# Front of a transformer tower: the patch stage one tile further ahead, two banks for turned queries and keys, the patch weights' sum by products

## The chip, the cores and the metric

The kernel runs on one core of one Trainium2 chip. The metric is the device time of one execution in microseconds (us). The core's engines are TensorE (PE in the profile; PEld is its weight load), VectorE (DVE), ScalarE (ACT), GpSimd (POOL) and SyncE (SP), which issues the DMAs. Each works through its own queue in order; semaphores order them among each other.

## The reference, cut to what matters

32 images of 96x96 are cut into 36 patches each. Patches are normalised, projected to 256 numbers, normalised again and given a position; with two class tokens an image has 38 tokens. Then come attention with ternary weights, a mixture of experts, attention in integers and three blocks with quantised weights. The change is in the first part and the first attention's projection:

```python
x = layernorm(x, ln1_g, ln1_b)                     # 1152 patches x 768
x = einsum('bhwp,pd->bhwd', x, W) + bias           # x 256
x = layernorm(x, ln2_g, ln2_b) + pe
h = concatenate([cls_tok, cls_token + cls_pos, x])
qkv = layernorm(h) @ ternary_weight(w_qkv).T
q, k = rms_norm(q), rms_norm(k)
q, k = rotary(q) * q_gain, rotary(k)
... softmax(q k^T) v, then @ ternary_weight(w_proj).T, the experts, the second layer
```

## The kernel before, in words

The tokens are 10 tiles of 128 (`NT`), the patches the first 9 of them (`TOK`). Item 0 of the second part is the tile of class tokens (`Z_TILE[0]` is tile 9), item n is tile n - 1. Normalisations are folded into weights: the patch weights, scaled by ln1's gain (`patch_c`), are centred by subtracting the mean over all 768 rows. VectorE adds the six row blocks up (`patch_total`), TensorE multiplies the total by ones (`patch_sums`, after 12 passes that sum ln1's bias rows), VectorE subtracts (`patch_weights`). VectorE also rounds the ternary weights, those of qkv first (`ternary_rounded(0)`, `ternary_made(0)`) and those of the output projection at the end of the front (part 1).

A patch tile t then goes this way: TensorE turns it (`patches_turned`, L621), ScalarE copies it to SBUF (`patches_kept`), TensorE projects it (`patches_projected`, L629, 12 passes into bank `Y`), VectorE makes y and its statistics (`y_stats`, L409), GpSimd the inverse root and shift (`y_rstd`, L579), ScalarE normalises (`normalised`, L733), GpSimd multiplies by the gain and adds the position (`placed`, L585 and L588: h is made). `embedded(part)` (L574) adds the bias row to three tiles of the position table; x's own statistics are `x_stats` and `x_rstd`.

Item n goes on: TensorE turns h (`rows_turned`), ScalarE copies (`rows_kept`), TensorE projects (`projected`, L650), ScalarE takes the values and the squares (`values`, `squared`), VectorE sums the squares and rotates (`z_rotated`, L431 first), GpSimd adds the rotated halves (`rotation_added`, L569), ScalarE takes the root (`rooted`), VectorE inverts and scales (`row_factor`, `row_scaled`), TensorE turns the row (`heads_turned`, L658, into bank `QK`), and ScalarE lays it out by image (`by_image`, L769 and L771). `h_stats` and `h_rstd` (L565) are the statistics of h.

Each engine has a loop written out by hand, `for i in range(NT + 1)`. In turn i it does the patch work of tile i, `rows_turned` to `squared` of item i, and `z_rotated` to `by_image` of item i - 1; turns 0 and 1 are special. The order in TensorE's turn is `patches_projected(i)`, `rows_turned(i)`, `patches_turned(i + 1)`, `projected(i)`, `heads_turned(i - 1)`. Scores of the first attention (L863) wait for `by_image` of the last item. Before the first load has landed, the engines have only memsets and ScalarE's table load.

## Time and profile before

| what | us |
|---|---|
| median of three runs (lowest, highest) | 539.51 (535.71, 540.89) |
| the profiled execution, device time | 536.86 |
| its span, first to last instruction | 535.0 |
| TensorE busy, share of the span | 412.5, 77% |
| VectorE busy | 315.0, 59% |
| ScalarE busy | 244.9, 46% |
| GpSimd busy | 155.0, 29% |
| mean granted TensorE clock, share of full | 0.865 |

The front is the first 93.8 us of the span. Durations and times of day below are of the profiled execution. Windows were read for the clock that TensorE was granted, timelines for who waits for whom; "[idle 2.15 <- ACT front L771]" on a row says that the engine stood still for 2.15 us ahead of it and that ScalarE's line 771 released it.

### The profile page before, as it was taken

To read this page: it belongs to the slowest core of one execution; us is meant where nothing else is said; L and a number is where in the kernel's file an instruction comes from. 1 tells how busy PE (TensorE), PEld (TensorE's weight loads), DVE (VectorE), ACT (ScalarE), POOL (GpSimd) and SP (SyncE) were. 2 spreads that over 40 slices of the span, in tenths; PEclk is the share of its full clock that TensorE was granted. 3 is DMA by queue.
4 is the path that set the end of the run, shared out by engine and by line. 5 is a ranking of instruction groups with operands and counts; after the bars stand their busy time and mean duration, and the time that the engine had idled before them with its cause. 6 is when DMAs were issued, how large, how long until landed. Compare 5 with 4: busy or idle time off the path is not lost.

```text
span 535.0 us, 9515 instructions
## 1 busy us (share of the span) xinstructions
PE 412.5 (77%) x3499; PEld 303.6 (57%) x3499; DVE 315.0 (59%) x846; ACT 244.9 (46%) x519; POOL 155.0 (29%) x191
## 2 busy tenths in 40 slices
PE   5678883577798999999889995532796147699997
PEld 3556652466687866665556783211343135589996
DVE  4977877789472311323321228669898997636643
ACT  4245544365745212222112212693298478566651
POOL 3485773689320610000000054008010001213310
PEclk9898997599988999999999998685555556999999
DMA  8941111970015140111110081000000000000002
GB/s 270 401 177 17 23 23 20 374 337 3 2 45 222 69 147 21 39 58 44 39 39 31 21 308 45 0 1 2 1 2 0 1 4 2 1 1 2 1 20 75
DMA packets 19793, 38.64 MB, mean 72 GB/s; under 512 B 2136, under 2 KB 16164, under 8 KB 18340
## 3 DMA queue, kind: packets, MB, share of 16 engines
q1 hardware_dynamic: 18788, 35.41, 19.2%
q0 software_dynamic: 960, 2.62, 1.4%
q8 instruction: 29, 0.48, 0.4%
q14 instruction: 16, 0.13, 0.1%
HBM read 29.77 MB, written 7.01 MB: 69 GB/s over the span
## 4 chain that ended last, share of the span: by engine, by line
PE 51%; DVE 24%; ACT 11%; issue 6%; POOL 4%; DMA 2%; DVEq 0%; SPq 0%; ACTq 0%; POOLq 0%
PE psum L1314 11%; PE psum L1346 5%; PE psum L1321 5%; PE psum L2406 4%; PE psum L2439 3%; PE psum L1360 3%; PE psum L985 2%; DVE ring L905 2%; ACT experts L1722 2%; PE psum L2445 2%; DVE att_den L912 2%; PE psum L1338 1%; DMA front<-expert_results,slot_of 1%; PE psum L2423 1%; DVE att_max L908 1%
## 5 line engine op out<-in xcount | busy, mean ns | idle before, releaser
L1314 PE MATMUL psum<-experts,ring 128*128 x136 | 64.3, 596 | 1.9 <-issue 1.2
L1138 DVE TENSOR_TENSOR ring<-ring,psum 128x512 f32<-128x512 f32 x17 | 11.7, 688 | 62.8 <-PE psum L1314 62.8
L1245 POOL DMA_INDIRECT front<-expert_results,slot_of x10 | 9.7, 974 | 125.0 <-DMA expert_results<-ring 122.2
L1321 PE MATMUL psum<-front,shared 128*128 128x256 f32 (+1 forms) x160 | 36.3, 382 | 0.0
L1314 PEld LDWEIGHTS psum<-experts,ring 128*128 128x128 f32 x136 | 23.3, 190 | 19.4 <-issue 19.4
L1321 PEld LDWEIGHTS psum<-front,shared 128*128 128x128 f32 x160 | 30.4, 197 | 3.7
L1346 PE MATMUL psum<-experts,ring 128*128 x136 | 32.1, 379 | 0.0
L1346 PEld LDWEIGHTS psum<-experts,ring 128*128 128x128 f32 x136 | 25.8, 190 | 10.3 <-issue 7.7
L2406 PE MATMUL psum<-experts 128*128 128x256 f32 (+1 forms) x120 | 27.5, 372 | 4.6 <-ACT experts L2469 4.6
L629 PE MATMUL psum<-experts,ring 128*128 128x256 f32 x108 | 27.6, 409 | 2.6 <-DVE ring L409 2.6
L1444 ACT COPY ring<-psum 128x512 f32<-128x512 f32 x17 | 10.0, 586 | 42.3 <-PE psum L1338 42.3
L2406 PEld LDWEIGHTS psum<-experts 128*128 128x128 f32 x120 | 21.8, 190 | 7.6 <-ACT experts L2469 5.4
L1430 ACT COPY ring<-psum 128x256 f32<-128x256 f32 x17 | 6.3, 372 | 42.8 <-PE psum L1330 42.8
L629 PEld LDWEIGHTS psum<-experts,ring 128*128 128x128 f32 x108 | 21.6, 206 | 6.4 <-issue 3.0
L873 PE MATMUL psum<-tab,experts 128*128 128x128 f32 x128 | 18.8, 295 | 6.4 <-ACT ring L935 6.3
L2479 ACT ACTIVATE ring<-psum,ffn_first_b 128x256 f32<-128x256 f32 (+1 forms) x30 | 12.3, 459 | 24.8 <-PE psum L2406 24.8
L2380 POOL TENSOR_TENSOR ffn_rs<-ffn_var,minus_half 128x2 f32<-128x2 f32 x15 | 10.4, 693 | 44.7 <-DVE ffn_var L2324 44.7
L1360 PE MATMUL psum<-shared,ring 128*128 128x256 f32 (+1 forms) x80 | 20.0, 405 | 3.8 <-DVE ring L1143 3.8
L2174 POOL TENSOR_TENSOR rstd<-out_var,minus_half 128x2 f32<-128x2 f32 x5 | 4.0, 796 | 63.4 <-DVE out_var L2135 63.4
L841 POOL TENSOR_TENSOR ring<-ring,att_max 128x608 f32<-128x608 f32 x16 | 19.3, 1209 | 7.1 <-DVE att_max L908 6.3
L1143 DVE TENSOR_TENSOR ring<-ring,psum 128x512 f32<-128x512 f32 (+1 forms) x10 | 6.6, 661 | 24.9 <-PE psum L1321 24.9
L846 POOL TENSOR_TENSOR experts<-experts,att_inv 128x608 f32<-128x608 f32 x16 | 19.4, 1211 | 2.3 <-DVE att_inv L916 2.3
(364 smaller groups left out, 1072.2 us busy)
## 6 DMA issues: line engine op xcount, KB each, us to landing
experts<-in_experts SPq DMA_DIRECT2D x8, 1536.0 KB, 12.1
experts<-in_x SPq DMA_DIRECT2D x9, 384.0 KB, 8.3
expert_rows<-zeros SPq DMA_DIRECT2D x1, 2176.0 KB, 14.6
ring<-expert_rows SPq DMA_DIRECT2D x17, 128.0 KB, 2.1
shared<-in_shared SPq DMA_DIRECT2D x1, 1536.0 KB, 17.7
experts<-in_ffn_q SPq DMA_DIRECT2D x1, 1536.0 KB, 6.4
experts<-in_ffn_s SPq DMA_DIRECT2D x1, 1536.0 KB, 10.7
experts<-in_pos_embed SPq DMA_DIRECT2D x1, 1152.0 KB, 9.4
```

The costliest lines, as they stand in the source:

```text
L629: mm = nc.tensor.matmul(psum[:, Y, 0:D], tok_xT[t % 2][:, k, :], patch_c[:, k, :], start=(k == 0), stop=(k == KP - 1))
L841: nc.gpsimd.tensor_tensor(att_s[p % 3], att_s[p % 3], m, ALU.subtract).then_inc(s_shifted.sem, 1)
L846: nc.gpsimd.tensor_tensor(att_p[p % 3][:, :, 0:SEQ], att_p[p % 3][:, :, 0:SEQ], w, ALU.mult).then_inc(p_scaled.sem, 1)
L873: tr = nc.tensor.transpose(psum[:, 4 + c // 4, (c % 4) * P:(c % 4 + 1) * P], att_p[p % 3][:, 2 * c:2 * c + 2, :], ident)
L1138: nc.vector.tensor_tensor(o, o, up_bank(g), ALU.mult).then_inc(hidden_done.sem, 1)
L1314: mm = nc.tensor.matmul(bank, sl_xT[t % 2][:, k, :], slot_w(t, block, k, F), start=(k == 0), stop=(k == KD - 1))
L1321: mm = nc.tensor.matmul(o[:, b, 0:w], shared_w(block, k, (2 * half + b) * P, P), moe_x(c)[:, k, 0:w], start=(k == 0), stop=(k == KD - 1))
L1346: mm = nc.tensor.matmul(psum[:, 2, 0:D], sl_hT[t % 2][:, k, :], slot_w(t, 2, k, D), start=(k == 0), stop=(k == KF - 1))
L1360: mm = nc.tensor.matmul(psum[0:m, 3, u * D:(u + 1) * D], sh_h[c % 2][:, k, u * P:u * P + m], shared_w(2, k, 0, D), start=(k == 0), stop=(k ...
L2406: mm = nc.tensor.matmul(psum[:, n % 2, o * CHUNK:o * CHUNK + w], ffn_w[:, 2 * b, k, o * P:(o + 1) * P], ffn_xT[:, k, a:a + w], start=(k == ...
L2439: mm = nc.tensor.matmul(psum[:, 6 + n % 2, o * CHUNK:o * CHUNK + w], ffn_w[:, 2 * b + 1, k, o * P:(o + 1) * P], g[:, k, 0:w], start=(k == ...
L2479: nc.scalar.activation(ffn_sq[n % 2][:, k, 0:w], psum[:, n % 2, k * CHUNK:k * CHUNK + w], ACT.Square, bias=ffn_first_b[:, b, k:k + 1])
```

## The change

The patch stage runs one tile further ahead. In turn i the engines now do the patch work of tile i + 1 (`patches_projected`, `y_stats`, `y_rstd`, `placed`, `normalised`) and turn tile i + 2, beside the items i and i - 1 as before. The turns 0 and 1 are written out. Turned queries and keys have two banks, 5 and 7, so that `heads_turned(n)` waits for `by_image(n - 2)` and not n - 1; the turned weights of the output projection go to bank 4. The patch weights' total is made in three sums of two blocks, one addition on VectorE, and TensorE adds the three up with products by ones. `embedded` has parts of 1, 2, 3 and 3 tiles instead of 3 x 3: the first waits for the ternary rounding of qkv, the others stand behind `x_rstd(2)`, `x_rstd(3)` and the end of turn 3. ScalarE begins with one square root of zeros. Nothing behind the front is changed.

```diff
@@ -343,7 +343,7 @@
...
         v_row = view(ring, 3840, 4, 2, KV_HEADS, 2, HD)
-        patch_t = tok_yn[1]
+        patch_t = view(ring, PATCH_DIM, KP // 2, D)
         x_mv, x_var, x_rs = sb("x_mv", [P, TOK, 2]), sb("x_var", [P, TOK]), sb("x_rs", [P, TOK])
...
@@ -368,8 +368,9 @@
...
         Z_TILE = [NT - 1] + list(range(NT - 1))
-        XT, Y, HT, Z, QK = 0, 2, 3, [4, 6], 5
-        TERN_QKV, TERN_PROJ, SUM, ROW = 6, 7, 7, 6
+        XT, Y, HT, Z, QK = 0, 2, 3, [4, 6], [5, 7]
+        TERN_QKV, TERN_PROJ, SUM, ROW = 6, 4, 7, 6
+        POS_PARTS = [range(0, 1), range(1, 3), range(3, 6), range(6, TOK)]
         TERN_COLS, TERN_GROUPS = [slice(0, 3 * D), slice(3 * D, 5 * D)], [slice(0, 12), slice(12, 20)]
...
@@ -490,7 +491,7 @@
...
                 dve.wait_ge(patch_scaled.sem, patch_scaled.done(0))
-                nc.vector.tensor_reduce(patch_t, patch_c.rearrange("p k d -> p d k"), AX.X, ALU.add).then_inc(patch_totaled.sem, 1)
+                nc.vector.tensor_tensor(patch_t, patch_c[:, 0:KP // 2, :], patch_c[:, KP // 2:KP, :], ALU.add).then_inc(patch_totaled.sem, 1)
 
...
@@ -524,26 +525,28 @@
...
             patch_rows()
-            for i in range(NT + 1):
+            y_stats(0)
+            ternary_made(0)
+            x_stats(1)
+            dve.wait_ge(cls_made.sem, cls_made.done(0))
+            h_stats(NT - 1)
+            x_stats(2)
+            y_stats(1)
+            qkv_weights()
+            h_stats(0)
+            y_stats(2)
+            x_stats(3)
+            for i in range(2, NT + 1):
                 for n in z_items(i - 1):
                     z_rotated(n)
-                if i == 1:
-                    dve.wait_ge(cls_made.sem, cls_made.done(0))
-                    h_stats(NT - 1)
-                    y_stats(i)
-                if 1 <= i <= TOK:
+                if i <= TOK:
                     h_stats(i - 1)
...
                     row_factor(n)
-                if i < TOK and i != 1:
-                    y_stats(i)
+                if i + 1 < TOK:
+                    y_stats(i + 1)
                 for n in z_items(i - 1):
                     row_scaled(n)
-                if i == 0:
-                    ternary_made(0)
-                    x_stats(1)
-                if i == 1:
-                    qkv_weights()
                 if i + 2 < TOK:
...
@@ -571,8 +574,9 @@
...
                 pool.wait_ge(l_pe.sem, l_pe.all)
-                nc.gpsimd.tensor_tensor(pos_embed[:, 3 * part:3 * part + 3, :], pos_embed[:, 3 * part:3 * part + 3, :],
-                                        rows[:, 1:2, :].to_broadcast((P, 3, D)), ALU.add).then_inc(pos_ready.sem, 1)
+                r = POS_PARTS[part]
+                nc.gpsimd.tensor_tensor(pos_embed[:, r[0]:r[-1] + 1, :], pos_embed[:, r[0]:r[-1] + 1, :],
+                                        rows[:, 1:2, :].to_broadcast((P, len(r), D)), ALU.add).then_inc(pos_ready.sem, 1)
 
...
@@ -584,30 +588,38 @@
...
                 pool.wait_ge(yn_scaled.sem, yn_scaled.done(t))
-                pool.wait_ge(pos_ready.sem, pos_ready.done(t // 3))
+                pool.wait_ge(pos_ready.sem, pos_ready.done([t in r for r in POS_PARTS].index(True)))
                 nc.gpsimd.tensor_tensor(h[:, t, :], tok_yn[t % 2], pos_embed[:, t, :], ALU.add).then_inc(h_made.sem, 1)
...
             x_rstd(0)
+            y_rstd(0)
+            pool.wait_ge(tern_ready.sem, tern_ready.done(0))
             embedded(0)
-            for i in range(NT + 1):
+            x_rstd(1)
+            placed(0)
+            h_rstd(NT - 1)
+            x_rstd(2)
+            embedded(1)
+            y_rstd(1)
+            placed(1)
+            h_rstd(0)
+            y_rstd(2)
+            placed(2)
+            x_rstd(3)
+            embedded(2)
+            for i in range(2, NT + 1):
                 for n in z_items(i - 1):
                     rotation_added(n)
-                if i == 1:
-                    h_rstd(NT - 1)
-                    y_rstd(i)
-                if 1 <= i <= TOK:
+                if i <= TOK:
                     h_rstd(i - 1)
-                if i < TOK and i != 1:
-                    y_rstd(i)
-                if i < TOK:
-                    placed(i)
-                if i == 0:
-                    x_rstd(1)
+                if i + 1 < TOK:
+                    y_rstd(i + 1)
+                    placed(i + 1)
                 if i + 2 < TOK:
                     x_rstd(i + 2)
-                if i in (0, 1):
-                    embedded(1 + i)
+                if i == 3:
+                    embedded(3)
             for u in range(3):
...
@@ -652,10 +664,10 @@
...
                 pe.wait_ge(row_made.sem, row_made.done(t))
-                if t >= 1:
-                    pe.wait_ge(qkT_ready.sem, qkT_ready.done(t - 1))
+                if t >= 2:
+                    pe.wait_ge(qkT_ready.sem, qkT_ready.done(t - 2))
                 for c in range(3):
-                    tr = nc.tensor.transpose(psum[:, QK, c * P:(c + 1) * P], qk_row[t % 2][:, c * P:(c + 1) * P], ident)
+                    tr = nc.tensor.transpose(psum[:, QK[t % 2], c * P:(c + 1) * P], qk_row[t % 2][:, c * P:(c + 1) * P], ident)
                 tr.then_inc(qkT_turned.sem, 1)
...
@@ -688,32 +700,35 @@
...
                 pe.wait_ge(patch_totaled.sem, patch_totaled.done(0))
-                nc.tensor.matmul(psum[:, SUM, 0:D], ones, patch_t, start=True, stop=True).then_inc(patch_summed.sem, 1)
+                for k in range(KP // 2):
+                    mm = nc.tensor.matmul(psum[:, SUM, 0:D], ones, patch_t[:, k, :], start=(k == 0), stop=(k == KP // 2 - 1))
+                mm.then_inc(patch_summed.sem, 1)
 
...
             patches_turned(0)
-            for i in range(NT + 1):
-                if i < TOK:
-                    if i == 0:
-                        patches_turned(1)
-                        pe.wait_ge(patch_centred.sem, patch_centred.done(0))
-                    patches_projected(i)
-                if i == 1:
-                    ternary_turned()
-                    rows_turned(0)
-                    ternary_summed()
-                    patches_turned(2)
-                    pe.wait_ge(qkv_centred.sem, qkv_centred.done(0))
-                    projected(0)
-                    rows_turned(1)
-                    projected(1)
-                elif i < NT:
-                    if i >= 2:
-                        rows_turned(i)
-                        if i + 1 < TOK:
-                            patches_turned(i + 1)
-                        projected(i)
+            pe.wait_ge(patch_centred.sem, patch_centred.done(0))
+            patches_projected(0)
+            patches_turned(1)
+            patches_projected(1)
+            ternary_turned()
+            rows_turned(0)
+            patches_turned(2)
+            ternary_summed()
+            patches_projected(2)
+            patches_turned(3)
+            pe.wait_ge(qkv_centred.sem, qkv_centred.done(0))
+            projected(0)
+            rows_turned(1)
+            projected(1)
+            for i in range(2, NT + 1):
+                if i + 1 < TOK:
+                    patches_projected(i + 1)
+                if i < NT:
+                    rows_turned(i)
+                    if i + 2 < TOK:
+                        patches_turned(i + 2)
+                    projected(i)
                 for n in z_items(i - 1):
...
@@ -764,7 +779,7 @@
...
                 s = slice(POS_TILE * t, POS_TILE * t + n)
-                bank = psum[:, QK, 0:QK_ROW].rearrange("p (c s i) -> p c s i", c=3, s=POS_TILE)[:, :, 0:n, :]
+                bank = psum[:, QK[item % 2], 0:QK_ROW].rearrange("p (c s i) -> p c s i", c=3, s=POS_TILE)[:, :, 0:n, :]
                 q_out = q_im[:, :, 0:IMAGES * SEQ].rearrange("p b (i s) -> p b s i", s=SEQ)[:, :, s, :]
...
@@ -776,6 +791,8 @@
...
 
+            act.wait_ge(zeros_ready.sem, zeros_ready.done(0))
+            nc.scalar.activation(qkv_sd[:, 0, :], zeros[:, 0:HK], ACT.Sqrt)
             act.wait_ge(l_patch_w.sem, l_patch_w.all)
...
@@ -785,31 +802,31 @@
...
             patches_kept(0)
-            for i in range(NT + 1):
+            patches_kept(1)
+            normalised(0)
+            ternary_taken(0)
+            rows_kept(0)
+            patches_kept(2)
+            normalised(1)
+            patches_kept(3)
+            values(0)
+            squared(0)
+            rows_kept(1)
+            normalised(2)
+            values(1)
+            squared(1)
+            for i in range(2, NT + 1):
                 for n in z_items(i - 1):
                     rooted(n)
-                if i < 2:
-                    if i == 1:
-                        ternary_taken(0)
-                        rows_kept(0)
-                    patches_kept(i + 1)
-                    normalised(i)
-                if i == 1:
-                    values(0)
-                    squared(0)
-                    rows_kept(1)
-                    values(1)
-                    squared(1)
-                if i >= 2:
-                    for n in z_items(i):
-                        rows_kept(n)
-                    if i + 1 < TOK:
-                        patches_kept(i + 1)
-                    if i < TOK:
-                        normalised(i)
-                    for n in z_items(i):
-                        values(n)
-                        squared(n)
+                if i < NT:
+                    rows_kept(i)
+                if i + 2 < TOK:
+                    patches_kept(i + 2)
+                if i + 1 < TOK:
+                    normalised(i + 1)
+                if i < NT:
+                    values(i)
+                    squared(i)
                 for n in z_items(i - 1):
...
             ternary_taken(1)
```

## Rows read from the trace of the kernel before

**Rows 1.** Timeline, one steady turn: start us, us, engine, line, operation [idle before <- releaser].
```profile
55.65 2.76 PE L629 MATMUL psum<-experts,ring 128*128 128x256 f32 x12
...
56.98 0.49 DVE L431 TENSOR_REDUCE qkv_ss<-experts 128x20 f32<-128x320 f32 x1 [0.40 <-ACT experts L752]
...
59.12 1.53 PE L650 MATMUL psum<-qkv_w,ring 128*128 128x384 f32 x4
...
59.40 0.48 DVE L409 SCALAR_TENSOR_TENSOR ring<-psum,x_rs,rows 128x256 f32<-128x256 f32 x1
...
60.83 0.71 POOL L579 TENSOR_TENSOR y_rs<-y_var,minus_half 128x1 f32<-128x1 f32 x1 [0.72 <-DVE y_var L416]
...
61.94 0.60 ACT L733 ACTIVATE ring<-ring,y_shift,y_rs 128x256 f32<-128x256 f32 x1 [1.77 <-POOL y_shift L581]
...
63.11 0.49 DVE L431 TENSOR_REDUCE qkv_ss<-experts 128x20 f32<-128x320 f32 x1 [0.41 <-ACT experts L752]
```

**Rows 2.** Windows: us, busy of PE, PEld, DVE, ACT, POOL, granted clock, DMA, GB/s.
```profile
42.50:43.40 0.90, 0.84 (x4) 0.87 (x5) 0.86 (x5) 0.00 (x0) 0.90 (x3) 0.50 0.11 30
...
56.10:62.20 6.10, 5.36 (x28) 4.08 (x27) 5.40 (x23) 3.59 (x12) 4.50 (x8) 1.00 0.17 23
```

**Rows 3.** Timeline, VectorE's L431 and TensorE around the third turn.
```profile
35.07 0.49 DVE L431 TENSOR_REDUCE qkv_ss<-experts 128x20 f32<-128x320 f32 x1 [1.35 <-ACT experts L752]
...
41.67 0.49 DVE L431 TENSOR_REDUCE qkv_ss<-experts 128x20 f32<-128x320 f32 x1
...
42.56 0.87 PE L658 MATMUL psum<-tab,ring 128*128 128x128 f32 x3 [2.15 <-ACT front L771]
...
43.23 3.89 PE L629 MATMUL psum<-experts,ring 128*128 128x256 f32 x12
...
50.86 0.48 DVE L431 TENSOR_REDUCE qkv_ss<-experts 128x20 f32<-128x320 f32 x1 [0.41 <-ACT experts L752]
```

**Rows 4.** Timeline, the front's last turns and the first scores.
```profile
81.47 0.48 DVE L431 TENSOR_REDUCE qkv_ss<-experts 128x20 f32<-128x320 f32 x1 [1.77 <-ACT experts L752]
...
83.47 2.93 PE L650 MATMUL psum<-qkv_w,ring 128*128 128x384 f32 x4 [0.46 <-ACT ring L739]
...
93.76 0.81 PE L863 MATMUL psum<-front 32*64 32x76 f32 x32 [0.79 <-ACT front L771]
```

**Rows 5.** Groups of instructions by form, 0 to 95 us: busy us, mean ns | idle before.
```profile
L569 POOL TENSOR_TENSOR experts<-experts 128x320 f32<-128x320 f32 x10 | 8.6, 863 | 7.1 <-DVE experts L436 7.1
...
L588 POOL TENSOR_TENSOR h<-ring,experts 128x256 f32<-128x256 f32 x9 | 6.6, 728 | 0.7
...
L574 POOL TENSOR_TENSOR experts<-experts,rows 128x768 f32<-128x768 f32 x3 | 5.8, 1918 | 3.5 <-DMA experts<-in_pos_embed 3.5
...
L565 POOL TENSOR_TENSOR rstd<-var_eps,minus_half 128x1 f32<-128x1 f32 x10 | 5.7, 568 | 0.0
...
L471 DVE TENSOR_SCALAR experts<-experts 128x512 int16<-128x512 bf16 x1 | 0.3, 294 | 0.0
```

**Rows 6.** Timeline, the start of the front.
```profile
8.78 2.78 DVE L493 TENSOR_REDUCE ring<-experts 128x256 f32<-128x1536 f32 x1 [1.36 <-ACT experts L781]
...
11.70 0.67 PE L691 MATMUL psum<-ring,tab 128*128 128x256 f32 x2
...
12.83 2.07 DVE L499 SCALAR_TENSOR_TENSOR experts<-psum,experts 128x256 f32<-128x256 f32 x6
...
17.08 2.13 POOL L574 TENSOR_TENSOR experts<-experts,rows 128x768 f32<-128x768 f32 x1 [3.46 <-DMA experts<-in_pos_embed]
...
17.58 1.84 DVE L471 TENSOR_SCALAR experts<-experts 128x768 int16<-128x768 bf16 x1
...
19.79 0.48 DVE L409 SCALAR_TENSOR_TENSOR ring<-psum,x_rs,rows 128x256 f32<-128x256 f32 x1
...
20.42 4.29 PE L629 MATMUL psum<-experts,ring 128*128 128x256 f32 x12 [2.61 <-DVE ring L409]
...
24.81 0.15 DVE L401 TENSOR_SCALAR x_var<-x_mv 128x1 f32<-128x1 f32 x1
```

## The prediction

> **What bounds the kernel now.** I read the chain of waits first: it goes through every stage, and the diff touches none behind the front. So the change is worth what it moves the moment at which attention can start, the first score product at 93.76 us of the span of 535.0 us. I take everything behind it to shift by the same amount.
>
> Then I read the timeline of one steady turn. I mark a turn by VectorE's reduction L431, the first instruction of `z_rotated(n)`, and call it z(n). z(4) is at 56.98, z(5) at 63.11: a turn is 6.13 us, and the chain in it is closed. From z(4) VectorE works 2.42 us (rotation, `h_stats`, `row_factor`) until `y_stats` starts (L409). 1.43 us later GpSimd starts y's power (L579), after 1.11 more ScalarE can normalise (L733), and behind that in its queue stand `values` and `squared`, whose end releases z(5) 1.17 later: 2.42 + 1.43 + 1.11 + 1.17 = 6.13 [rows 1]. VectorE is busy 5.40 of 6.10 us, TensorE 5.36, GpSimd 4.50 in 8 instructions [rows 2].
>
> Two places are off this beat. z(2) to z(3) is 50.86 - 41.67 = 9.19 us, 3.06 more than a turn: the second `heads_turned` waits 2.15 us for its only bank, which ScalarE is still emptying, and behind that pause the projection L629 takes 3.89 us [rows 3] instead of 2.76 [rows 1]. The granted clock was 0.50, its lower level, as the wait ended [rows 2]. And the tail, where little is left to overlap: z(8) at 81.47, scores at 93.76 [rows 4].
>
> **The change, part by part.**
>
> *Steady turn: 0.* In turn i the patch work of tile i+1 stands where that of i stood, and on every engine the kinds of work keep their order. `squared(i)` is still behind a normalisation, which waits for GpSimd, which waits for VectorE in the same turn: the 6.13 us chain is as long as before. x's factor is now made only one turn ahead; its power ends before the 2.42 us at which `y_stats` wants it, since GpSimd's work behind z is `placed`'s rest and one power (0.73 + 0.57) [rows 5].
>
> *Two banks: -2.9.* The 2.15 us wait goes, and with it the pause that the slow projection followed: -3.06 for z(2) to z(3), and +0.14 as both `by_image` now stand ahead of `rooted(2)` on ScalarE. If the projection stays slow though the wait goes, about -2.0; the lower end is 0, where ScalarE's queue and not the bank holds the turn.
>
> *Patch weights' sum: +0.5.* VectorE's strided reduction took 2.78 us, but TensorE came to its product only at 11.70, behind the row products, just as the reduction ended [rows 6]. So a quicker addition releases nobody, whatever it takes below 2.78. TensorE now makes three products, four more passes. A pass of this width is 2.76/12 = 0.23 us in a steady projection [rows 1], 0.36 in the slow one at 20.42 [rows 6]: +0.9 to +1.4. I take 0.9, since L691's two passes took 0.67 in all, so its end goes from 12.37 to 13.3. L499 started at 12.83, when VectorE came free [rows 6]; now at 13.35.
>
> *GpSimd out of the way of the rounding: -1.4.* L471 with 768 elements took 1.84 us [rows 6], with 512 elements 0.29 [rows 5], which makes 0.44 for 768. While the long one ran, GpSimd was in `embedded(0)`, from 17.08 to 19.21 [rows 6]; the short one ran alone. Now `embedded(0)` waits for `tern_ready`. The bounds are 0 and -1.4.
> The Trainium skill (SBUF — State Buffer, Terms) says that VectorE and GpSimd arbitrate for one port pair, held to the end of an instruction. By that rule L471 stood still until GpSimd's addition was over, which these rows agree with; were the width alone at work, the term would be 0 and the total 1.4 us later.
>
> With both, x's statistics for tile 1, which ended at 24.96 [rows 6], end at about 24.1.
>
> *GpSimd's queue in the new prologue: +1.6.* Here I see the gain go. The embedding additions (3 x 1.92 us [rows 5]) were made where no chain hung on GpSimd for long. Now they stand, as 1, 2, 3 and 3 tiles, between the steps of the y chain. From 24.1, with a power 0.57, `h_rstd` with its small product 0.8, `placed` twice 0.73 and a gap 1.5, a rotation 0.87, three tiles 1.81, two tiles 1.25 (between 0.73 and 1.81) [rows 5], y's pair 1.0 and ScalarE's normalisation 0.65 (1.11 and 0.60 with their gaps [rows 1]): x(1) 0.57, placed(0) 1.5, h(9) 0.8, x(2) 0.57, two tiles 1.25, y(1) 1.0, ScalarE 0.65, placed(1) 1.5, h(0) 0.8, y(2) 1.0, ScalarE 0.65, placed(2) 1.5, x(3) 0.57, three tiles 1.81, two rotations 1.74, h(1) 0.8, y(3) 1.0. That is 17.71; with a few gaps y(3)'s shift is ready at 42.0, and z(2) comes 1.17 behind the normalisation's start, at 43.2 against 41.67.
> TensorE alone would be sooner. It has one patch projection more ahead of z(1), +2.76; it starts its prologue 0.9 earlier, and the projection at 20.42 took 4.29 us behind a pause [rows 6] which is now shorter: 2.76 - 0.9 - 1.4 = +0.5. z(1) would be at 35.6, and VectorE goes from z(1) to z(2) in 6.6 us [rows 3]: z(2) at 42.2. The slower of the two queues counts.
>
> *embedded(3), at the end of turn 3: +1.1.* It puts 1.81 us between x's power and `rotation_added(3)`. GpSimd is idle for 0.72 us ahead of L579 in a turn [rows 1], so y(5) is 1.81 - 0.72 = 1.1 late, and all behind it. The bounds are 0 and 1.8.
>
> *Tail: -0.8.* In turn 8 no y work is left: z(8) needs `rows_kept(8)`, the projection and ScalarE's two squares. In a steady turn that projection starts 2.14 us behind z (59.12) [rows 1]; here no patch projection is ahead of its turned rows, and I take 1.7. It took 1.53 us there [rows 1] and 2.93 after a thin stretch [rows 4]. TensorE will have had about 0.9 us of work in the 4 us ahead of it, so I take 2.93, and 0.7 for the squares (1.17 less the normalisation's share): 1.7 + 2.93 + 0.7 = 5.33 instead of 6.13. Bounds: -0.4 with 2.14, -2.2 at the high clock. From z(8) to the scores it is 12.29 us [rows 4], VectorE's own work with the rounding of the last weights first, then one tile alone: as before.
>
> *ScalarE's early square root: 0.* The table load ahead of the first `rooted` lay beside VectorE's rotation and `h_stats`; it goes under the wait for the weights, with one small activation.
>
> **The sum.** z(2) +1.6 (which has the first two terms of the start in it); banks -2.9: z(3) at 49.6, -1.3; embedded(3) +1.1: z(4) at 56.8, -0.2; tail -0.8: scores at about 92.8. In all **-1.0**. The profiled execution took 536.86 us with its span of 535.0, so 535.9 by its own account. It lies 2.65 below the median of the three runs, 539.51; all four have a mean of 538.24. I put the forecast on that: 537.2.
>
> **The rivals.**
> 1. *GpSimd's queue hides after all*, its instructions lying under other waits: z(2) +0.5, banks -2.9, embedded(3) 0, tail -0.8 to -2.2: -3.2 to -4.6, so 533.6 to 535.0. For it: GpSimd is idle 1.6 us of a turn [rows 2]. Against: the additions come as one piece of 1.81.
> 2. *Slower, by TensorE's new order.* `projected(0)` and `projected(1)` stand behind `patches_projected(2)` and `patches_turned(3)`. At the lower level the two patch projections there cost 1.1 to 1.5 more each and the two of h 1.4 each, some 5.2 us, of which 1.1 is hidden beside GpSimd's queue (43.2 against 42.2); the total is -1.0 + 4.1 = +3.1, 541.3. It turns the sign from a delay of 2.1 us on. For it: a projection right behind a pause was slow twice [rows 3, 6]. Against: the pauses there are now about 1 us.
> 3. *The bank did not hold turn 3*: ScalarE's two `by_image` do. The total is -1.0 + 2.9 = +1.9, 540.1. Against: the row names what TensorE waited for, the bank's last reader [rows 3], and with a second bank nothing else is ahead of that transpose.
>
> **How the numbers follow.** The forecast's case has 0.50 (535.7 to 538.7), rival 1 0.27, rival 2 0.13, rival 3 0.10. About 1%, 5.4 us, is what a measurement of this kernel can tell from no change. No case reaches it alone. Faster by over 1% needs rival 1 with the high clock in the tail and some more: 0.13; slower by over 1% needs rivals 2 and 3 together: 0.06; within 1%: 0.81. The range reaches from rival 1 with a fast execution to rival 2: 532.5 to 541.0.
>
> **What the profile after would show.** L471 at 768 elements near 0.44 us; the first L409 at 18.9; no wait of L658 for ScalarE and z(2) to z(3) near 6.3; z(2) near 43.2, with GpSimd hardly idle from 24 to 42; z(3) to z(4) near 7.2, the other turns 6.13; z(7) to z(8) near 5.3; scores near 92.8. The prediction is wrong if z(2) is ahead of 42.5 or behind 45, if z(3) to z(4) is 6.1, or if a stage behind the scores changes its length by over 1 us.

## The result, and the profile after

The changed kernel takes 533.19 us (median of 9 runs, 530.27 to 535.75) against 537.87 (9 runs, 535.71 to 540.89); the ratio is 0.9917, 95% interval 0.9892 to 0.9941. So it is faster by 0.8%, 3 to 6 us. Its profiled execution took 535.75 us with a span of 533.9, its slowest run: one pair of executions shows 1.1 us, the medians 4.7. How far that can be accounted for is told below.

| moment in the front, us | before | forecast | after |
|---|---|---|---|
| first `y_stats` | 19.79 | 18.9 | 18.14 |
| z(2) | 41.67 | 43.2 | 41.76 |
| z(3) | 50.86 | 49.6 | 47.89 |
| z(4) | 56.98 | 56.8 | 54.88 |
| z(8) | 81.47 | 80.5 | 77.76 |
| z(9) | 88.60 | - | 84.89 |
| first scores | 93.76 | 92.8 | 90.06 |

The scores start 3.70 us earlier, not 1.0. Line numbers have moved: L431 is now L432, L409 L410, L471 L472, L499 L500, L574 L578, L579 L583, L629 L641, L650 L662, L658 L670, L691 L704, L739 L754, L752 L767, L771 L786, L863 L880; in the variants below a line can be off by one or two more.

The start of the front, timeline of the changed kernel (start us, us, engine, line, operation, idle before); it answers to [rows 6]:

```profile
10.94 1.27 PEld L704 LDWEIGHTS psum<-ring,tab 128*128 128x128 f32 x6
...
11.15 1.46 PE L704 MATMUL psum<-ring,tab 128*128 128x256 f32 x6
...
12.65 2.08 DVE L500 SCALAR_TENSOR_TENSOR experts<-psum,experts 128x256 f32<-128x256 f32 x6 [1.46 <-PE psum L704]
...
17.41 0.36 DVE L472 TENSOR_SCALAR experts<-experts 128x768 int16<-128x768 bf16 x1
...
18.14 0.48 DVE L410 SCALAR_TENSOR_TENSOR ring<-psum,x_rs,rows 128x256 f32<-128x256 f32 x1
...
22.03 0.73 POOL L578 TENSOR_TENSOR experts<-experts,rows 128x256 f32<-128x256 f32 x1 [0.54 <-DVE experts L482]
...
23.16 0.15 DVE L402 TENSOR_SCALAR x_var<-x_mv 128x1 f32<-128x1 f32 x1
...
25.98 2.83 PE L641 MATMUL psum<-experts,ring 128*128 128x256 f32 x12 [1.02 <-DVE ring L410]
```

VectorE's sum is ready before TensorE gets to the three products, and `patch_weights` (L500) waits 1.46 us for them, yet starts at 12.65 against 12.83. The rounding L472 takes 0.36 us instead of 1.84. The second patch projection takes 2.86 us at 19.24, the third 2.83: no slow one, where [rows 6] has 4.29.

GpSimd's additions (L578) and y's power (L583) in the new prologue, VectorE's L444 and L422 beside them, and the two transposes L670:

```profile
26.67 1.26 POOL L578 TENSOR_TENSOR experts<-experts,rows 128x512 f32<-128x512 f32 x1
...
35.40 1.82 POOL L578 TENSOR_TENSOR experts<-experts,rows 128x768 f32<-128x768 f32 x1
35.43 0.42 DVE L422 BATCH_NORM_STATS2 hst<-h 128x6 f32<-128x256 f32 x1
...
36.47 0.79 DVE L444 TENSOR_TENSOR qkv_rg<-qkv_rg,gain 128x20 f32<-128x20 f32 x1
...
39.55 0.56 POOL L583 TENSOR_TENSOR y_rs<-y_var,minus_half 128x1 f32<-128x1 f32 x1
...
39.95 1.08 PE L670 MATMUL psum<-tab,ring 128*128 128x128 f32 x6 [1.67 <-DVE ring L458]
...
41.76 0.49 DVE L432 TENSOR_REDUCE qkv_ss<-experts 128x20 f32<-128x320 f32 x1
```

GpSimd waited three times 0.72 us for ScalarE's normalisation between 24 and 42, 2.2 us in all, and for nothing else. L444 is a product of 128x20 that takes 0.18 us in a steady turn; here it takes 0.79, until the addition at 35.40 is over. Not every VectorE instruction is held: L422 at 35.43 took its usual 0.42 us beside the same addition. The six passes of the transposes now run together and wait for VectorE's row alone; the wait of 2.15 us for ScalarE in [rows 3] is gone.

Turn 3 to 4, and the tail; they answer to [rows 1] and [rows 4]:

```profile
47.89 0.48 DVE L432 TENSOR_REDUCE qkv_ss<-experts 128x20 f32<-128x320 f32 x1 [0.41 <-ACT experts L767]
...
49.42 1.80 POOL L578 TENSOR_TENSOR experts<-experts,rows 128x768 f32<-128x768 f32 x1
...
50.19 1.07 DVE L444 TENSOR_TENSOR qkv_rg<-qkv_rg,gain 128x20 f32<-128x20 f32 x1
...
52.75 0.57 POOL L583 TENSOR_TENSOR y_rs<-y_var,minus_half 128x1 f32<-128x1 f32 x1
...
54.88 0.48 DVE L432 TENSOR_REDUCE qkv_ss<-experts 128x20 f32<-128x320 f32 x1 [0.41 <-ACT experts L767]
```

```profile
73.25 0.49 DVE L432 TENSOR_REDUCE qkv_ss<-experts 128x20 f32<-128x320 f32 x1 [1.77 <-ACT experts L767]
...
74.79 2.25 PE L662 MATMUL psum<-qkv_w,ring 128*128 128x384 f32 x4 [2.49 <-ACT ring L754]
...
77.76 0.49 DVE L432 TENSOR_REDUCE qkv_ss<-experts 128x20 f32<-128x320 f32 x1 [1.35 <-ACT experts L767]
...
84.89 0.48 DVE L432 TENSOR_REDUCE qkv_ss<-experts 128x20 f32<-128x320 f32 x1
...
90.06 0.81 PE L880 MATMUL psum<-front 32*64 32x76 f32 x32 [0.80 <-ACT front L786]
```

z(2) to z(3) is 6.13 us (9.19 in [rows 3]), z(3) to z(4) 6.99, the turns after it 6.12, turn 8 4.51, z(8) to z(9) 7.13 and from there to the scores 5.17.

What I had not looked at is TensorE in the prologue. The windows of the changed kernel, then those of the kernel before (us, busy of PE, PEld, DVE, ACT and POOL with counts, granted clock, DMA share, GB/s):

```profile
15.00:31.00 16.00, 13.99 (x72) 10.57 (x71) 14.67 (x47) 4.97 (x11) 9.17 (x14) 1.00 1.06 411
...
31.00:45.00 14.00, 11.43 (x56) 8.78 (x57) 12.10 (x46) 7.78 (x26) 12.10 (x21) 1.00 0.18 40
```

```profile
15.00:31.00 16.00, 10.99 (x45) 8.10 (x46) 15.20 (x42) 4.00 (x8) 10.39 (x14) 0.89 1.06 410
...
31.00:45.00 14.00, 10.25 (x44) 7.30 (x43) 10.25 (x42) 7.98 (x24) 10.77 (x17) 0.90 0.20 47
```

From 15 to 31 us TensorE now is busy for 13.99 us instead of 10.99 and keeps its granted clock of 1.00 up to 45 us, where before it fell to a mean of 0.89 and 0.90, that is, for a part of the time to its lower level of 1.2 GHz. The second of these falls stood behind the wait for the bank [rows 2, 3]; the first is the one that goes with the order.

### The profile page after: what moved, and what is told of

Its sections match the earlier page's. It is cut to its first block, busy times and chain, and to the rows that moved or that the text cites. A ratio compares the mean times of both kernels' runs of the same rounds, so it can differ in the third digit from the quotient of the medians.

```text
span 533.9 us, 9523 instructions
## 1 busy us (share of the span) xinstructions
PE 413.0 (77%) x3502; PEld 305.2 (57%) x3503; DVE 313.8 (59%) x846; ACT 243.6 (46%) x519; POOL 154.4 (29%) x192
## 4 chain that ended last, share of the span: by engine, by line
PE 56%; DVE 22%; ACT 11%; issue 6%; POOL 3%; DMA 1%; DVEq 0%; SPq 0%; ACTq 0%; POOLq 0%
PE psum L1331 11%; PE psum L1338 6%; PE psum L1363 6%; PE psum L2423 4%; PE psum L1377 4%; PE psum L2456 3%; PE psum L890 2%; PE psum L2462 2%; PE psum L1002 2%; PE psum L1355 1%; ACT experts L1739 1%; PE psum L2440 1%; DVE tile_peak L1767 1%; DVE front L1766 1%; PE psum L641 1%
## 5 line engine op out<-in xcount | busy, mean ns | idle before, releaser
L1331 PEld LDWEIGHTS psum<-experts,ring 128*128 128x128 f32 x136 | 23.3, 190 | 19.5 <-issue 19.4
L1363 PEld LDWEIGHTS psum<-experts,ring 128*128 128x128 f32 x136 | 25.8, 190 | 10.3 <-issue 7.6
L641 PE MATMUL psum<-experts,ring 128*128 128x256 f32 x108 | 25.1, 382 | 3.5 <-DVE experts L500 1.5
L641 PEld LDWEIGHTS psum<-experts,ring 128*128 128x128 f32 x108 | 19.9, 190 | 7.1 <-DVE experts L500 1.8
L890 PEld LDWEIGHTS psum<-tab,experts 128*128 128x128 f32 x128 | 16.1, 158 | 9.1 <-POOL experts L863 8.3
L662 PE MATMUL psum<-qkv_w,ring 128*128 128x384 f32 x40 | 17.4, 563 | 5.0 <-ACT ring L754 5.0
```

The costliest lines, as they stand in the source:

```text
L641: mm = nc.tensor.matmul(psum[:, Y, 0:D], tok_xT[t % 2][:, k, :], patch_c[:, k, :], start=(k == 0), stop=(k == KP - 1))
L662: mm = nc.tensor.matmul(psum[:, Z[n % 2], 0:QKV], qkv_hT[n % 2][:, k, :], qkv_w[:, k, :], start=(k == 0), stop=(k == KD - 1))
L890: tr = nc.tensor.transpose(psum[:, 4 + c // 4, (c % 4) * P:(c % 4 + 1) * P], att_p[p % 3][:, 2 * c:2 * c + 2, :], ident)
L1331: mm = nc.tensor.matmul(bank, sl_xT[t % 2][:, k, :], slot_w(t, block, k, F), start=(k == 0), stop=(k == KD - 1))
L1363: mm = nc.tensor.matmul(psum[:, 2, 0:D], sl_hT[t % 2][:, k, :], slot_w(t, 2, k, D), start=(k == 0), stop=(k == KF - 1))
```

## The experiments

Where no median is given, a kernel was executed once. The first loads land up to 0.3 us apart, and the weights' centring ends at different times after them, so I compare lengths within a run: first `y_stats` less `patch_weights`, turns, and so on. All marks, in us:

| kernel | patch_weights | first y_stats | z(2) | z(2) to z(3) | z(3) to z(4) | turn 8 | z(8) to z(9) | scores |
|---|---|---|---|---|---|---|---|---|
| before | 12.83 | 19.79 | 41.67 | 9.19 | 6.12 | 6.12 | 7.13 | 93.76 |
| after | 12.65 | 18.14 | 41.76 | 6.13 | 6.99 | 4.51 | 7.13 | 90.06 |
| after, again | 13.04 | 18.54 | 42.15 | 6.12 | 7.00 | 3.86 | 7.14 | 89.80 |
| one_bank | 12.78 | 18.27 | 41.86 | 10.63 | 6.99 | 5.17 | 7.14 | 95.32 |
| reduce | 12.69 | 18.17 | 41.77 | 6.11 | 7.00 | 5.17 | 7.13 | 90.70 |
| emb0_early | 13.10 | 18.98 | 42.60 | 6.13 | 6.99 | 4.20 | 7.14 | 90.59 |
| spread | 13.07 | 18.55 | 41.17 | 6.12 | 6.12 | 5.17 | 7.14 | 89.25 |
| b_two_banks | 12.64 | 19.61 | 41.49 | 6.13 | 6.12 | 6.11 | 7.14 | 90.52 |
| b_two_banks, timed | 12.87 | 19.95 | 44.96 | 6.13 | 6.12 | 6.12 | 7.14 | 94.01 |
| round_early | 13.24 | 18.74 | 42.35 | 6.12 | 7.00 | 3.75 | 5.55 | 88.82 |
| no_sqrt | 11.90 | 17.39 | 40.99 | 6.12 | 6.99 | 4.96 | 7.14 | 89.73 |
| kept_busy | 13.15 | 18.65 | 42.24 | 6.12 | 6.99 | 3.79 | 7.14 | 89.81 |
| both | 13.54 | 19.03 | 41.65 | 6.12 | 6.12 | 4.76 | 5.18 | 88.45 |
| all3 | 12.55 | 18.04 | 40.66 | 6.13 | 6.12 | 3.76 | 4.92 | 86.56 |

**One bank again in the changed kernel (one_bank).**

```diff
-        XT, Y, HT, Z, QK = 0, 2, 3, [4, 6], [5, 7]
+        XT, Y, HT, Z, QK = 0, 2, 3, [4, 6], [5, 5]
...
-                if t >= 2:
-                    pe.wait_ge(qkT_ready.sem, qkT_ready.done(t - 2))
+                if t >= 1:
+                    pe.wait_ge(qkT_ready.sem, qkT_ready.done(t - 1))
```

> The changed kernel with one bank for turned queries and keys again. My theory (the bank holds turn 3): after, z(2) 41.76 and z(3) 47.89 are 6.13 us apart; here TensorE waits about 2 us for ScalarE's last copy ahead of the second heads_turned, the projection behind it is slow, and z(2) to z(3) is again near 9 us; scores near 93.0 instead of 90.06. Rival (ScalarE's queue of two by_image holds the turn, or being a tile ahead has already covered the bank): z(2) to z(3) stays within 0.5 us of 6.13 and scores at 90 to 90.5.

z(2) to z(3) is 10.63 us, 4.50 more than with two banks, and more than the 9 I expected. The timeline shows the wait of 2.16 us, and a patch projection L641 of 5.33 us behind it, for which `y_stats` waits 3.38:

```profile
42.76 0.88 PE L670 MATMUL psum<-tab,ring 128*128 128x128 f32 x3 [2.16 <-ACT front L786]
...
43.42 5.33 PE L641 MATMUL psum<-experts,ring 128*128 128x256 f32 x12
...
48.79 0.48 DVE L410 SCALAR_TENSOR_TENSOR ring<-psum,x_rs,rows 128x256 f32<-128x256 f32 x1 [3.38 <-PE psum L641]
...
52.49 0.49 DVE L432 TENSOR_REDUCE qkv_ss<-experts 128x20 f32<-128x320 f32 x1 [0.40 <-ACT experts L767]
```

The bank held the turn. Nearly all beyond the wait is the slow projection, 2.6 us over its steady 2.75. Turn 8 is 5.17.

**Two banks alone on the kernel before (b_two_banks).**

```diff
-        XT, Y, HT, Z, QK = 0, 2, 3, [4, 6], 5
-        TERN_QKV, TERN_PROJ, SUM, ROW = 6, 7, 7, 6
+        XT, Y, HT, Z, QK = 0, 2, 3, [4, 6], [5, 7]
+        TERN_QKV, TERN_PROJ, SUM, ROW = 6, 4, 7, 6
```

(with the wait for t - 2 and the bank by item, as in the change)

> The kernel before with two banks for turned queries and keys and nothing else. Theory (the bank is worth 2.9 us by itself, whatever the patch stage does): z(2) 41.7 as before, z(3) at 47.9 instead of 50.86, scores at 90.8 instead of 93.76. Rival (the bank alone only moves the wait on to ScalarE): z(3) after 49.5.

```profile
39.69 1.08 PE L658 MATMUL psum<-tab,ring 128*128 128x128 f32 x6 [0.68 <-DVE ring L457]
...
41.49 0.49 DVE L431 TENSOR_REDUCE qkv_ss<-experts 128x20 f32<-128x320 f32 x1
...
47.62 0.49 DVE L431 TENSOR_REDUCE qkv_ss<-experts 128x20 f32<-128x320 f32 x1 [0.40 <-ACT experts L752]
```

The wait for ScalarE is gone, z(2) to z(3) falls to 6.13 and nothing else moves: scores at 90.52, 3.24 of the 3.70 us. Timed:

> The kernel before with two banks alone, timed. Theory from the looks (the bank is 3.1 of the 3.7 us by which the scores moved; the rest of the change gives 1.5 back at the start, costs 1.7 in the new prologue and 0.9 in turn 3, and gains 1 to 2 in turn 8): 3 to 3.5 us under before, that is within 1.5 us of the changed kernel. Rival (the changed order is the main gain): at most 1.5 us under before.

534.64 us, median of 12 runs, ratio to before 0.9951 (0.9921 to 0.9981). Timed beside it, the changed kernel took 531.72 us, median of 7, ratio 0.9905 (0.9872 to 0.9938), and the kernel before 535.64, median of 20:

> The changed kernel once more, so that the next three can be compared with it on one chip: 4 to 5 us under the kernel before, as it was (533.19 against 537.87), scores at 90.1 +- 0.6 by when the first loads land.

So the bank alone gives 0.5% and the whole change 0.8 to 1.0%. I had expected the bank alone to be 3 to 3.5 us under before and within 1.5 us of the changed kernel; both were missed. It is 1.0 us under before by the medians and 2.4 by the means, and 2.9 or 2.3 us behind the changed kernel. The two intervals against before overlap a little, but the 12 and the 7 times can be compared directly: the difference of their means, 2.3 us, has a 95% interval of about 1.0 to 3.7. So the rest of the change helps too, by about as much as the bank, though the marks of the first pair left it 0.5 us. The profiled execution of the timed kernel says where such a rest can come from. The first execution of the two-bank kernel, with the projections of h and VectorE's marks:

```profile
29.93 1.56 PE L650 MATMUL psum<-qkv_w,ring 128*128 128x384 f32 x4 [1.86 <-DVE qkv_w L512]
...
34.89 0.49 DVE L431 TENSOR_REDUCE qkv_ss<-experts 128x20 f32<-128x320 f32 x1 [1.35 <-ACT experts L752]
...
41.49 0.49 DVE L431 TENSOR_REDUCE qkv_ss<-experts 128x20 f32<-128x320 f32 x1
```

and the later one, the same program:

```profile
30.27 2.93 PE L650 MATMUL psum<-qkv_w,ring 128*128 128x384 f32 x4 [2.85 <-DVE qkv_w L512]
...
34.33 2.93 PE L650 MATMUL psum<-qkv_w,ring 128*128 128x384 f32 x4 [0.71 <-ACT ring L739]
...
37.97 0.49 DVE L431 TENSOR_REDUCE qkv_ss<-experts 128x20 f32<-128x320 f32 x1 [2.72 <-ACT experts L752]
...
44.96 0.48 DVE L431 TENSOR_REDUCE qkv_ss<-experts 128x20 f32<-128x320 f32 x1
```

Their windows, the first execution, then the later one:

```profile
31.00:45.00 14.00, 12.40 (x61) 9.26 (x60) 11.13 (x46) 8.92 (x27) 10.58 (x16) 1.00 0.20 45
...
31.00:45.00 14.00, 13.29 (x45) 8.85 (x44) 8.21 (x35) 6.20 (x19) 7.96 (x12) 0.69 0.17 46
```

The same program is at z(2) 3.5 us later. Both projections of h took 2.93 us instead of 1.56, z(1) came at 37.97 instead of 34.89, and the granted clock from 31 to 45 us was 0.69 (1.00 in the first execution). The old order has pauses of 2.6 us ahead of the second patch projection and 1.7 to 2.9 us ahead of the first projection of h; at which of them the clock falls differs from execution to execution: in the first one the projection behind 2.6 us took 4.09 us and those of h 1.56, in the later one it took 2.83 and those of h 2.93. z(2) less the first `y_stats` is 21.88 us in two executions with the old order and 25.01 in this one. In the eleven executions with the new order it is 23.6, or 22.6 where the additions are spread, and never anything else.

**The patch weights' sum as before (reduce).**

```diff
-                nc.vector.tensor_tensor(patch_t, patch_c[:, 0:KP // 2, :], patch_c[:, KP // 2:KP, :], ALU.add).then_inc(patch_totaled.sem, 1)
+                nc.vector.tensor_reduce(patch_t[:, 0, :], patch_c.rearrange("p k d -> p d k"), AX.X, ALU.add).then_inc(patch_totaled.sem, 1)
...
-                for k in range(KP // 2):
-                    mm = nc.tensor.matmul(psum[:, SUM, 0:D], ones, patch_t[:, k, :], start=(k == 0), stop=(k == KP // 2 - 1))
+                for k in range(1):
+                    mm = nc.tensor.matmul(psum[:, SUM, 0:D], ones, patch_t[:, k, :], start=True, stop=True)
```

> The changed kernel with VectorE's strided reduction and one product for the patch weights' total again. The prediction as written (the reduction is covered by TensorE's row products, three products cost 0.9 more): first y_stats 0.5 us earlier than in the changed kernel (17.6 instead of 18.14). Theory after reading both traces (the weight load of the product stood idle for 0.64 us for the reduction, which the matmul rows hide): patch_weights starts 0.2 us later (12.85 instead of 12.65) and the first y_stats too, at 18.3; z(2) 41.9, scores 90.2.

```profile
11.53 0.50 PEld L704 LDWEIGHTS psum<-ring,tab 128*128 128x128 f32 x2 [0.64 <-issue]
...
12.69 1.41 DVE L500 SCALAR_TENSOR_TENSOR experts<-psum,experts 128x256 f32<-128x256 f32 x4
```

ScalarE's first scaling to `patch_weights` is 6.59 us here (6.10 to 12.69) and 6.59 before (6.24 to 12.83), where VectorE was busy with the reduction and x's statistics behind it until it came to L500. With the three products it is 6.32 in the changed kernel's first profile and 5.80 to 7.26 over all ten, 6.73 in the mean: the products take 1.46 to 1.93 us, and the row products ahead of them end earlier or later. So this part moves the start by -0.8 to +0.7 us, by how fast TensorE runs there, and by +0.1 in the mean; the 0.2 us in favour of the products, which I expected here, were those of one execution.

**GpSimd's first addition early (emb0_early).**

```diff
+            embedded(0)
             y_rstd(0)
-            pool.wait_ge(tern_ready.sem, tern_ready.done(0))
-            embedded(0)
```

> The changed kernel with GpSimd's first position addition (one tile) made as soon as its tables are in, not behind the ternary rounding. Theory (VectorE's 768-element rounding stands still while a GpSimd addition runs): the addition of one tile takes 0.73 us and lies from about 17.1 to 17.9, so the rounding instruction takes 0.36 plus what it overlaps, 0.7 to 0.9 us, and the first y_stats comes 0.3 to 0.6 later than 18.14. In return GpSimd has 0.73 less behind the rounding. Rival (the long instruction of before was long by its size): it stays at 0.36 us and the kernel gains up to 0.7 us at z(2).

```profile
16.21 0.72 POOL L578 TENSOR_TENSOR experts<-experts,rows 128x256 f32<-128x256 f32 x1 [4.53 <-DMA experts<-in_pos_embed]
...
16.39 0.57 DVE L466 TENSOR_SCALAR tern_scale<-tern_sum 128x12 bf16<-128x12 f32 x1
...
18.25 0.36 DVE L472 TENSOR_SCALAR experts<-experts 128x768 int16<-128x768 bf16 x1
```

The addition came earlier than I thought, at 16.21, and so the rounding L472 took 0.36 us all the same. It is L466, a small scaling of 0.17 us in the changed kernel, that now took 0.57 and ended with the addition. First `y_stats` less `patch_weights` is 5.88 instead of 5.49: +0.4, in the range I gave, by another instruction than I named.

**Additions as single tiles in GpSimd's waits (spread).**

```diff
+        POS_PARTS = [range(t, t + 1) for t in range(TOK)]
...
             y_rstd(1)
+            embedded(1)
             placed(1)
...
                 if i + 1 < TOK:
                     y_rstd(i + 1)
+                    embedded(i + 1)
                     placed(i + 1)
...
-                if i == 3:
-                    embedded(3)
```

(`embedded(2)` likewise stands behind `y_rstd(2)`, and the two- and three-tile parts of the prologue are gone)

> The changed kernel with the position additions cut into single tiles, each behind y's shift, where GpSimd waits 0.72 us for ScalarE's normalisation. Theory (the 2 and 3 tile additions stand in the y chain, by GpSimd's queue and by the port that VectorE's additions of two SBUF inputs want): z(3) to z(4) falls from 6.99 to 6.13, z(2) is 0.8 to 1.3 earlier, scores 88.0 to 88.5 instead of 90.06. Rival (GpSimd has no part in it, VectorE's own work sets both): scores at 90.1. Third: the single additions hold up row_scaled on VectorE in each turn, and turns grow to 6.3 or more: scores at 90 or later.

```profile
46.06 0.73 POOL L578 TENSOR_TENSOR experts<-experts,rows 128x256 f32<-128x256 f32 x1
...
47.29 0.49 DVE L432 TENSOR_REDUCE qkv_ss<-experts 128x20 f32<-128x320 f32 x1 [0.40 <-ACT experts L766]
```

z(3) to z(4) is 6.12, and no turn is longer than that: the addition of 0.73 us fits into the wait for ScalarE. z(2) less `patch_weights` is 28.10 instead of 29.11, 1.0 earlier. z(1) less `patch_weights` is 21.5 in both kernels, so the two-tile addition at 26.67 cost nothing and all of the 1.0 lies between z(1) and z(2) (6.60 instead of 7.60), beside the three-tile addition. So the additions in large pieces cost 1.0 + 0.87 us. Whether GpSimd's queue or VectorE's held L444 did it, this edit does not separate, as it takes both away: in the changed kernel L444 was held for 0.61 and 0.42 us ahead of z(2) and for 0.89 us ahead of z(4), which is the whole of either loss, and GpSimd came to y's power 0.2 us behind VectorE's statistics both times. The scores, at 89.25, are 0.8 earlier and not the 1.6 expected at the least, because turn 8 was 5.17 here and 4.51 there, and the start 0.4 later.

**Without the early square root (no_sqrt).** The edit takes out the two lines that the change adds ahead of ScalarE's first wait.

> The changed kernel without ScalarE's early square root. Theory (the table load ahead of the first rooted is covered): a load of 1.28 us stands near 34.2, row_factor starts up to 0.9 later than 36.17, because VectorE's h_stats ends at 36.25 and the load would end at 35.45: 0 to 0.3 us at z(2), scores 90.1 to 90.4. Rival (it delays rows_kept and the projection behind it): scores at 91.0 or later.

```profile
33.54 1.28 ACT L775 ACT_TABLE_LOAD   x1
...
34.83 0.51 ACT L775 ACTIVATE qkv_sd<-qkv_ss,eps_var 128x20 f32<-128x20 f32 x2
```

The load stands there, ends at 34.82, and the root starts 0.01 later. z(2) less `patch_weights` is 29.09, against 29.11: nothing.

**The first half of the last rounding in turn 7 (round_early).**

```diff
+                if i == TOK - 2:
+                    ternary_rounded(1)
                 if i == TOK:
-                    ternary_rounded(1)
                     ternary_made(1)
```

> The changed kernel with the first half of the output weights' ternary rounding (2.2 us on VectorE) moved from the end of turn 9 to the end of turn 7, where VectorE idles 1.77 us. Theory (VectorE's own work is what sets z(8) to z(9), 7.13 us, until TensorE and ScalarE take over at 5.1): z(7) 0.4 later (73.7), z(8) 78.2, z(9) 5.1 to 5.4 behind it, at 83.3 instead of 84.89, scores 88.5. Rival (the slow projection holds z(9) in any case): z(9) stays at 84.9 or moves by the 0.4 only.

z(8) to z(9) is 5.55 instead of 7.13, so VectorE's own work had set it; I had expected 5.1 to 5.4. Turn 7 grew from 6.13 to 6.78, and the scores are at 88.82.

**TensorE kept at work in the tail (kept_busy).**

```diff
-                for k in range(KD):
+                for k in list(range(KD)) * (5 if n >= NT - 2 else 1):
                     tr = nc.tensor.transpose(psum[:, HT, k * P:(k + 1) * P], h[:, t, k * P:(k + 1) * P], ident)
```

> The changed kernel with the transposes of the last two rows repeated five times (the same values into the same bank), to give TensorE work in the pause ahead of the projections of items 8 and 9. Theory (those projections are slow only because the clock fell in that pause): the projection of item 8 takes 1.56 us instead of 2.25 and z(8) comes 0.6 earlier (77.1 instead of 77.76); the rest moves with it, scores 89.4. Rival (the clock falls all the same, since transposes of 0.4 us each are too thin): z(8) unchanged at 77.8 or later by the longer transposes.

Turn 8 is 3.79 us with both projections at 1.56. But the second execution of the changed kernel had a turn 8 of 3.86 without it, and round_early 3.75, so one execution proves nothing for kept_busy alone. What the executions show together is that turn 8 has two ends, 3.8 with the projection at 1.56 to 1.78 and 5.17 with 2.93, and values between.

**The gains together (both, all3).** Spread and round_early, and then kept_busy as well.

> The changed kernel with the position additions as single tiles behind y's shift and the first half of the last rounding in turn 7. Theory (the two gains add: 1.9 at z(4), 1.1 to 1.6 at z(9)): scores 86.5 to 87.5 instead of 90.06, and the time 3 us under the changed kernel, 7 to 8 under before. Rival (behind the scores the gain is lost to other waits): under 1.5 us better than the changed kernel.

> The last one with the repeated transposes of the last two rows as well. Theory (at the high clock in turns 8 and 9 the projection chain shortens, and z(8) to z(9) is TensorE's chain once the rounding is out of it): turn 8 at 3.8 us, z(8) to z(9) under 5.5, scores 85 to 86.5. Rival (the clock falls in this gap anyway, or the longer transposes eat it): scores as without, at 86.5 to 87.5.

both: scores at 88.45, expected 86.5 to 87.5; 531.70 us, median of 8, ratio 0.9911 (0.9875 to 0.9948): no better than the changed kernel's 531.72 beside it, where I expected 3 us; the rival (less than 1.5 us) came. Its turn 7 took 7.56 us, as VectorE's rounding and GpSimd's additions got in each other's way; L466 alone takes 0.17 us and L470 0.69, and GpSimd's L593 0.73:

```profile
71.11 0.65 DVE L466 TENSOR_SCALAR tern_scale<-tern_sum 128x8 bf16<-128x8 f32 x1
...
72.03 1.00 DVE L470 TENSOR_TENSOR experts<-experts,tern_inv 128x512 bf16<-128x512 bf16 x1
...
72.56 1.05 POOL L593 TENSOR_TENSOR h<-ring,experts 128x256 f32<-128x256 f32 x1
```

all3: scores at 86.56, 528.95 us, median of 6 (527.87 to 531.26), ratio to before 0.9860 (0.9823 to 0.9898). It is the fastest of all, 1.4% under before and 2.8 us under the changed kernel's median, whose runs began at 529.76 (means compared directly: 2.6 us, 95% interval about 1.1 to 4.2). Both projections in its tail are at the high clock:

```profile
73.84 1.56 PE L662 MATMUL psum<-qkv_w,ring 128*128 128x384 f32 x4 [2.65 <-ACT ring L754]
...
78.03 1.56 PE L662 MATMUL psum<-qkv_w,ring 128*128 128x384 f32 x4 [0.49 <-ACT ring L754]
```

z(8) to z(9) is 4.92 and turn 8 3.76, against 5.18 and 4.76 for both. That the repeated transposes did it is what I expected and what these two profiles agree with. But from `patch_weights` to the scores all3 is only 0.9 us shorter than both (74.01 against 74.91), and its median is 2.75 us lower; kept_busy alone was not timed. So where the larger part of all3's gain comes from stays open.

**Behind the scores.** From the first scores to the first row scattered to the experts, a stretch whose code no kernel changed, the 14 profiled executions took 79.8 to 83.5 us: 82.85 before, 83.50 in the changed kernel's first profile, 80.17 in its second. From 140 to 165 us the granted clock was 0.92 in the changed kernel's first profile and 1.00 in its second. In the first pair of profiles the lead is 3.70 us at the scores, 3.05 at the scatter and 1.1 at the end; most of that loss lies behind 362 us, in stages that no kernel changed either, and I did not find its cause. Such differences are of the size of the spread of about 1% between the runs of one program.

## Why the prediction was right, and where it was not

The time, 533.19 us, lies in the range, 0.7 us from its lower end, and the change is within 1%, as I thought likeliest, though its interval reaches to 1.1%. But the forecast's own case (-1.0 us, 535.7 to 538.7) did not come: the range held because it reached down to rival 1, whose size the measured 3 to 6 us have, and rival 1's reason is right only in part. At the scores, z(2) was +0.1 and not +1.6, the banks -3.1 and not -2.9, embedded(3) +0.9 and not +1.1, the tail -1.6 and not -0.8: -3.7 in place of -1.0, and of the 2.7 between them the prologue has 1.5 and the tail 0.8. Two of my own signs of being wrong came true: z(2) at 41.76 is ahead of 42.5, and from the scores to the end the lead shrank by 2.6 us, where I had taken everything behind the scores to shift by one amount. The second sign was badly chosen, as the stretch from the scores to the scatter alone differs by up to 3.7 us between executions. Two slips in rival 2 change nothing: 43.2 against 42.2 is 1.0 and not 1.1, and its 541.3 lies above the range's end of 541.0.

*Steady turn, 0.* Right: 6.12 us before and after.

*Two banks, -2.9.* The mechanism is shown by both experiments. It is -3.06 on the kernel before and 4.50 in the changed one, where the patch projection behind the wait is slower still. The +0.14 for ScalarE's two layouts was not there: the turn is 6.13.

*Patch weights' sum, +0.5.* The step that failed is "a quicker addition releases nobody". I read it off the matmul rows, and the ends of matmuls are modelled. The weight load of the product, in the timeline of the kernel before, shows it:

```profile
11.67 0.30 PEld L691 LDWEIGHTS psum<-ring,tab 128*128 128x128 f32 x2 [0.64 <-issue]
```

TensorE had ended the row products' loads at 11.03 and stood idle for 0.64 us, until the reduction was over at 11.56. That is more than the +0.5 of the term: -0.3 from the first scaling in this pair of profiles, +0.1 in the mean of the ten.

*Rounding, -1.4.* Right: first `y_stats` less `patch_weights` went from 6.96 to 5.49, -1.47. That a VectorE instruction stands still while GpSimd's addition runs was shown three more times: L466 until the addition's end in emb0_early, L444 at 36.47, and L444 at 50.19, which took 1.07 us and ended at 51.26, the addition at 51.22. The Trainium skill (SBUF — State Buffer, Terms) has it as one port pair for the two engines, held for a whole instruction; the trace agrees, with small VectorE instructions held for up to 0.9 us. Some of them are held and not all: L422 above was not.

*GpSimd's queue in the prologue, +1.6.* The sum was 17.7 us from x's statistics to y(3)'s shift; measured it is 17.3 (23.31 to 40.57). I added 0.2 for gaps that were not there, and the start of the sum came 0.8 sooner by the two terms above. My other queue was off too: z(1) came at 34.16 and not at 35.6, and z(1) to z(2) took 7.60 us and not 6.6. So z(2) was +0.1 and not +1.6. That the additions cost something there holds, at 1.0 us (spread), but not as I named it: y's statistics were ready at 39.34, just 0.2 us before GpSimd began with y(3). Both queues were late together, VectorE because its L444 was held up twice (0.79 and 0.60 us instead of 0.18); I had counted only GpSimd's.

*embedded(3), +1.1.* 0.87, and gone when spread. The size is near; of the reason (GpSimd's queue alone) the same holds as above, as L444 stood still for 0.89 us there.

*Tail, -0.8.* The slow end is 5.17 us, where I had 5.33. I took the slow projection, with the high clock as the other bound; the clock fell within or ahead of that projection in some executions and not in others, so the term is -0.95 to -2.3. In this profile it was -1.6.

*What was left out.* I took the prologue of before for fixed. It depends on at which pause TensorE's clock falls, and that is worth 3.1 us at z(2), counted from the first `y_stats`, for one and the same program. The new order had a granted clock of 1.00 from 15 to 31 us in all of its eleven executions, one_bank included, and from 31 to 45 in all but one_bank. It has the turned tiles and projections of three patches between the ternary steps, which is the likely reason. My rival 2 had this with the wrong sign. It would explain that medians differ by more than the marks of one pair, but how often the old order falls into the late case was not measured, and so it stays open how much of the 0.3 to 0.5% beyond the banks is due to it.

## What to carry to other kernels

A bank that is read by another engine's queue can cost more than the wait: behind the pause the next projection paid again (in one_bank 2.16 us of wait, a granted clock of 0.50 from 43.4 to 46.8 us, and 2.6 us more of projection). Two banks alone gave 3.2 of the 3.7 us at the scores in one pair of executions, but only about half of the change by the timed runs. Look at the weight loads' idle time and not only at the matmuls' to see what TensorE waits for. Put GpSimd's bulk work as small pieces into its waits for ScalarE, away from VectorE's instructions on SBUF; that shortened the front by 1.9 us in single executions, and no timed run shows it by itself. Judge a gain of under 1% by many runs of both kernels side by side: a single execution moves by as much, and the median of the kernel before was 537.87 in one series and 535.64 in the other.

## What the runs showed of the hardware that I had not expected

- One program, with the old order's pauses in its prologue, gave z(1) at 34.89 and at 37.97 us in two executions, with the granted clock at 1.00 or 0.69 from 31 to 45 us.
- A VectorE instruction of 0.17 us (L466) took 0.57 us over 12 columns and 0.65 over 8 when a GpSimd addition ran, so even small ones can be held; L422 took its usual 0.42 us beside one.
- The square root ran 0.01 us behind the end of its table load of 1.28 us.
